# Grouped convolution by block-Toeplitz matmuls inside an FFN kernel: both parts of the conv weights in one stationary

## What is computed

```python
# x (128, 32, 512), conv weight (32, 8, 9), 4 groups of 8 channels, cond (128, 128)
out = conv1d(x, weight, padding=4, groups=4)            # along the 512 places
h = out + (cond @ c_weight.T)[:, :, None] + bias[None, :, None]
up   = h.reshape(-1, 512) @ W_up.T                       # 1376 columns
gate = silu(h.reshape(-1, 512) @ W_gate.T)
y = x + (gate * up @ W_down.T).reshape(x.shape)
```

## Time and profile before

| | us |
|---|---|
| median of 3 runs | 750.9 (750.73 to 751.24) |
| the profiled execution | 751.72 |
| its span on the core | 749.9 |
| TensorE busy | 739.6 (99%) |
| VectorE busy | 379.5 (51%) |
| ScalarE busy | 274.4 (37%) |
| granted TensorE clock | 0.999 of full |

### The profile page before, as it was taken

The page is one execution under the profiler, slowest core; times in us unless marked ns, Lnnn a source line. Parts: engine busy times, 40 slices in busy tenths (PEclk is TensorE's granted clock), DMA queues, the critical chain, the costliest instruction groups (busy, mean ns, idle before and its releaser), DMA issues.

```text
span 749.9 us, 10087 instructions
## 1 busy us (share of the span) xinstructions
PE 739.6 (99%) x3375; PEld 602.4 (80%) x3375; DVE 379.5 (51%) x639; ACT 274.4 (37%) x521; POOL 52.4 (7%) x88
## 2 busy tenths in 40 slices
PE   7999999999999999999999999999999999999998
PEld 6778888878888888887888888887888888887886
DVE  3896766654765454436734545443753333334224
ACT  4565655543433233234322333324431332333221
POOL 4433323210000000000000000000000000000000
PEclk9999999999999999999999999999999999999999
DMA  6496578569977677765544866866443967775413
GB/s 186 114 317 239 187 273 281 186 226 327 354 268 247 216 222 219 197 205 159 167 135 171 282 202 193 244 194 180 162 133 106 312 190 196 194 193 172 141 29 112
DMA packets 115029, 152.37 MB, mean 203 GB/s; under 512 B 12482, under 2 KB 50530, under 8 KB 114978
## 3 DMA queue, kind: packets, MB, share of 16 engines
q1 hardware_dynamic: 114496, 151.51, 64.8%
q10 hardware_dynamic: 482, 0.21, 0.1%
HBM read 108.95 MB, written 34.34 MB: 191 GB/s over the span
## 4 chain that ended last, share of the span: by engine, by line
PE 94%; DVE 2%; DMA 1%; SPq 1%; issue 1%; ACT 1%; POOL 0%; POOLq 0%; DVEq 0%
PE bank L727 55%; PE bank L790 32%; PE bank L645 3%; PE bank L640 3%; SPq L344 1%; PE bank L683 1%; DVE hc_lo L1091 1%; DMA x_in<-in_x 1%; PE bank L606 1%; PE bank L654 1%; PE bank L665 0%; DMA stage<-g_all 0%; DVE g_all L1294 0%; DVE ring L1091 0%; DVE g_all L1192 0%
## 5 line engine op out<-in xcount | busy, mean ns | idle before, releaser
L727 PE MATMUL bank<-hc_hi,ring 128*128 128x512 f32 (+1 forms) x1204 | 374.0, 392 | 1.0 <-issue 1.0
L727 PEld LDWEIGHTS bank<-hc_hi,ring 128*128 128x128 f32 (+1 forms) x1204 | 221.4, 185 | 50.2 <-issue 1.4
L727 PE MATMUL bank<-hc_lo,ring 128*128 128x512 f32 (+1 forms) x602 | 234.8, 390 | 0.0
L790 PE MATMUL bank<-ring,g_hi 128*128 128x512 f32 (+1 forms) x704 | 218.6, 392 | 0.0
L790 PEld LDWEIGHTS bank<-ring,g_hi 128*128 128x128 f32 (+1 forms) x704 | 131.2, 188 | 28.1 <-DVE g_lo L1091 0.8
L859 ACT ACTIVATE mix<-bank 128x512 f32<-128x512 f32 (+1 forms) x129 | 76.7, 594 | 188.0 <-PE bank L727 188.0
L790 PE MATMUL bank<-ring,g_lo 128*128 128x512 f32 (+1 forms) x352 | 137.1, 390 | 0.0
L727 PEld LDWEIGHTS bank<-hc_lo,ring 128*128 128x128 f32 (+1 forms) x602 | 111.5, 185 | 25.8
L1091 DVE TENSOR_TENSOR g_lo<-g_all,g_hi 128x512 fp32r<-128x512 f32 (+1 forms) x88 | 60.4, 689 | 88.6 <-ACT g_hi L859 88.6
L859 ACT ACTIVATE g_hi<-g_all 128x512 fp32r<-128x512 f32 (+1 forms) x88 | 55.1, 629 | 114.1 <-PE bank L790 114.0
L1265 DVE TENSOR_TENSOR mix<-bank,mix 128x512 f32<-128x512 f32 (+1 forms) x43 | 29.7, 691 | 129.4 <-PE bank L727 129.4
(11 more groups left out here) (141 smaller groups left out, 468.7 us busy)
## 6 DMA issues: line engine op xcount, KB each, us to landing
ring<-saved SPq DMA_DIRECT2D x319, 256.0 KB, 3.0
saved<-ring SPq DMA_DIRECT2D x99, 256.0 KB, 3.7
g_all<-in_x SPq DMA_DIRECT2D x32, 256.0 KB, 3.6
out_y<-g_all SPq DMA_DIRECT2D x32, 256.0 KB, 3.7
x_in<-in_x SPq DMA_DIRECT2D x96, 64.0 KB, 2.1
stage<-win SPq DMA_DIRECT2D x96, 64.0 KB, 2.9
w_nat<-in_L_ffn_W_gate SPq DMA_DIRECT2D x10, 256.0 KB, 3.4
w_nat<-in_L_ffn_W_up SPq DMA_DIRECT2D x10, 256.0 KB, 3.4
```

Of the source, the lines that this page charges most:

```text
L727: mm = pe.matmul(bank[0:w, :], wt, hv, start=fresh and q == 0 and t == 0, stop=q == 1 and t == 2, skip_group_check=not fresh)
L790: mm = pe.matmul(acc(half, tt)[:], gs, wd, start=f == 0 and t == 0, stop=f == FC - 1 and t == 2)
```

## The change

It touches groups 2 and 3 (`PAIRED = 2`); group 1 keeps its six matmuls. The stationary of 128 columns now holds the high part of the weights for 8 places of output (64 columns) and the low part of the same (64 columns): `pair_even` is high and low, `pair_odd` low and high, both views of one tile `conv_t`. For 8 places of output, 16 places of input are enough, the matmul's 128 rows. One step is two banks: `conv_ps` gets the first 8 places of each window from `x` at the window's place with `pair_even`, `xt_ps` the second 8 from `x` shifted by 8 places with `pair_odd`; each by two matmuls, one with the high and one with the low part of `x`. Half of a bank is then the part with the high weights, the other half that with the low, and VectorE adds both (and with them the fourth product, low times low, which the kernel before left out).

For that, `turn_x` transposes twice per step (at the place, and 8 places on), into `x_turn` of 1024 columns; `split_pairs` splits 1024 columns at once on both engines; `read_pairs` is four sums of 64 partitions instead of one of 128, where the third and the fourth take up what the first two wrote; `read_head` is two. `x_in` gets 8 places more on either side: rows loaded are 544 bytes instead of 512 except for the last chunk, GpSimd writes zeros at the end (`pad_x`). The paired step stands ahead of product 3, not behind it. On VectorE `read_pairs(k - 1)` and `split_pairs(k)` stand ahead of `up_b`, and `turn_x(k + 1)` behind it; on ScalarE `split_pairs` stands behind product 2's copy and the SiLU.

```diff
 def load_x(grp, i):
     if grp > 0:
+        size = P + HALO if paired(grp) and i < KC - 1 else P
...
+            def paired_step(grp, k):
+                pe.wait_ge(xt_lo_done, STEPS * grp + k + 1)
+                pe.wait_ge(conv_out, CPG * grp + k + 1)
+                for half, (bank, t) in enumerate(((conv_ps, pair_even), (xt_ps, pair_odd))):
+                    for n, v in enumerate(xt(grp)):
+                        mm = pe.matmul(bank[:], t, v[:, half * WB * P:(half + 1) * WB * P], start=n == 0, stop=n == 1)
+                mm.then_inc(conv_done, 1)
...
                     product(g, f, 2)
+                    if conv and 1 <= k <= STEPS and paired(g + 1):
+                        paired_step(g + 1, k - 1)
                     product(g, f, 3)
-                    if conv and 1 <= k <= STEPS:
+                    if conv and 1 <= k <= STEPS and not paired(g + 1):
                         conv_step(g + 1, k - 1)
...
+            def read_pairs(grp, k):
+                i = k // 2
+                if k % 2 == 0:
+                    dve.wait_ge(staged[(i - 1) % KC], STAGED * (grp if i == 0 else grp + 1))
+                dve.wait_ge(conv_done, CPG * grp + k + 2)
+                lower, upper = slice(0, HALF), slice(HALF, P)
+                halves = ((conv_ps, lower, upper), (xt_ps, upper, lower))
+                w0 = k % 2 * WB
+                to = [windows(grp, i)[mine, w0:w0 + WB, :] for _, mine, _ in halves]
+                for n, (bank, mine, other) in enumerate(halves):
+                    dve.tensor_tensor(to[n], bank[other, :].rearrange("p (w n) -> p w n", w=WB),
+                                      ctxb[other, grp:grp + 1, :].broadcast_to([HALF, WB, P]), ALU.add).then_inc(conv_lo_out, 1)
+                for n, (bank, mine, other) in enumerate(halves):
+                    dve.wait_ge(conv_lo_out, (2 * STEPS + 2) * (grp - PAIRED) + 2 * k + n + 2)
+                    last = dve.tensor_tensor(to[n], bank[mine, :].rearrange("p (w n) -> p w n", w=WB), to[n], ALU.add)
...
+            def split_pairs(grp, k):
+                dve.wait_ge(xt_hi_done, STEPS * grp + k + 1)
+                last = lo(xt_lo[:, 0:2 * WB * P], x_turn[:], xt_hi[:, 0:2 * WB * P])
...
-                    if conv and 0 <= k < STEPS:
+                    if conv and 0 <= k < STEPS and (k == 0 or not paired(g + 1)):
                         turn_x(g + 1, k)
                     gate_a(n, f)
...
+                    if conv and 1 <= k <= STEPS and paired(g + 1):
+                        read_pairs(g + 1, k - 1)
                     if conv and 0 <= k < STEPS:
-                        split_x(g + 1, k)
+                        (split_pairs if paired(g + 1) else split_x)(g + 1, k)
...
                     up_b(n, f)
...
+                    if conv and 0 <= k < STEPS - 1 and paired(g + 1):
+                        turn_x(g + 1, k + 1)
                     up_a(n, f)
```

More of the change, by code:

```diff
@@ L126, in adaln_ffn @@
         xt_lo = sb("xt_lo", [P, (2 * WB + 1) * P], F32R)
-        x_in = sb("x_in", [P, CG, P])
-        x_blk = sb("x_blk", [P, WB, R, CG])
+        x_in = sb("x_in", [P, CG, HALO + P + HALO])
+        x_turn = sb("x_turn", [P, 2 * WB * P])
         win = sb("win", [P, JJ, P])
@@ L132, in adaln_ffn, with paired @@
         toep = sb("toep", [P, G, QN, CG])
[L133 to L136, removed]
+        conv_t = sb("conv_t", [P, 4 * P], F32R)
         ident = sb("ident", [P, P])
         copy0, copy2, copy4, act_a, act_b = (mix[:, n, :] for n in range(5))
+        x_blk = x_turn[:, 0:WB * P].rearrange("n (b r c) -> n b r c", b=WB, r=R)
+        ta_hi, ta_lo, tb_hi, tb_lo = (conv_t[:, n * P:(n + 1) * P] for n in range(4))
+        PAIRED = 2
+        HALF = P // 2
+        pair_even, pair_odd = conv_t[:, 0:P], conv_t[:, HALF:HALF + P]
+        def paired(grp):
+            return grp >= PAIRED
         def down_nat(f):
@@ L206, in adaln_ffn @@
         x_turned = sem("x_turned")
+        x_padded = sem("x_padded")
+        conv_lo_out = sem("conv_lo_out")
         xt_hi_done = sem("xt_hi_done")
@@ L296, in x_place @@
         def x_place(grp, i):
-            return x_first[:, i - 1] if grp == 0 and i > 0 else x_in[:]
+            return x_first[:, i - 1] if grp == 0 and i > 0 else x_in[:, :, HALO:HALO + P]
         def blocks(grp, k):
@@ L310, in adaln_ffn @@
         NB, CQ = P // QUAD, CG // (P // QUAD)
-        x_turn = x_blk[:, :, :, :].rearrange("n b r c -> n (b r c)")
         def x_split_from(grp, k):
-            return xt_bank(grp, k)[:] if grp == 0 else x_turn
+            return xt_bank(grp, k)[:] if grp == 0 else x_turn[:, 0:WB * P]
         def xt_at(grp, k):
@@ L352, in load_x @@
                 if grp > 0:
+                    size = P + HALO if paired(grp) and i < KC - 1 else P
                     for quad in range(NB):
                         for c in range(CQ):
-                            sp.dma_start(x_in[quad * QUAD:(quad + 1) * QUAD, c::CQ, :],
-                                         x[:, grp * CG + quad * CQ + c, i * P:(i + 1) * P].rearrange("(b n) l -> n b l", b=NB)
+                            sp.dma_start(x_in[quad * QUAD:(quad + 1) * QUAD, c::CQ, HALO:HALO + size],
+                                         x[:, grp * CG + quad * CQ + c, i * P:i * P + size].rearrange("(b n) l -> n b l", b=NB)
                                          ).then_inc(x_loaded, LD)
@@ L531, in mix_t_lo, with pad_x @@
                                        ALU.subtract).then_inc(w_made[kind], 1)
+            def pad_x(grp):
+                pool.wait_ge(x_turned, STEPS * grp + STEPS - 2)
+                pool.memset(x_in[:, :, HALO + P:], 0.0).then_inc(x_padded, 1)
             def mix_h_first(q):
@@ L549, in _ @@
             pool.tensor_copy(reorder[:].rearrange("p (m r) -> p m r", r=R), ident[:].rearrange("p (r m) -> p m r", r=R)).then_inc(consts, 1)
+            pool.memset(x_in[:, :, 0:HALO], 0.0).then_inc(consts, 1)
             wrap(1)
@@ L561, in _ @@
                         mix_t_lo(f + 1)
+                    if g + 1 < G and paired(g + 1) and f == STEPS - 1:
+                        pad_x(g + 1)
         @block.tensor
@@ L629, in conv_head @@
                     pe.wait_ge(conv_out, CPG * grp)
-                for n, (t, v) in enumerate(terms(tb_hi, tb_lo, *xt(grp))):
-                    mm = pe.matmul(conv_ps[:, 0:P], t[:], v[:, 0:P], start=n == 0, stop=n == 2)
+                if paired(grp):
+                    for n, v in enumerate(xt(grp)):
+                        mm = pe.matmul(conv_ps[:, 0:P], pair_odd, v[:, 2 * WB * P:], start=n == 0, stop=n == 1)
+                else:
+                    for n, (t, v) in enumerate(terms(tb_hi, tb_lo, *xt(grp))):
+                        mm = pe.matmul(conv_ps[:, 0:P], t[:], v[:, 0:P], start=n == 0, stop=n == 2)
+                mm.then_inc(conv_done, 1)
[3 more added lines that the diff above has]
+                for half, (bank, t) in enumerate(((conv_ps, pair_even), (xt_ps, pair_odd))):
+                    for n, v in enumerate(xt(grp)):
+                        mm = pe.matmul(bank[:], t, v[:, half * WB * P:(half + 1) * WB * P], start=n == 0, stop=n == 1)
                 mm.then_inc(conv_done, 1)
@@ L870, in split_toep @@
                     act.wait_ge(toep_done, 3)
+                if paired(grp):
+                    for at in (0, P):
+                        last = hi(conv_t[:, at:at + HALF], toep[:, grp:grp + 1, HALO:2 * HALO, :])
+                    last.then_inc(t_hi_done, 1)
+                    return
                 hi(ta_hi[:], toep[:, grp:grp + 1, HALO:QN, :])
                 hi(tb_hi[:, TB0:P], toep[:, grp:grp + 1, 0:HALO, :]).then_inc(t_hi_done, 1)
+            def split_pairs(grp, k):
+                act.wait_ge(conv_done, CPG * grp + (k + 1 if k > 0 else 0))
+                act.wait_ge(x_turned, STEPS * grp + k + 1)
+                last = hi(xt_hi[:, 0:2 * WB * P], x_turn[:])
+                if k == 0:
+                    last = hi(xt_hi[:, 2 * WB * P:], head[:])
+                last.then_inc(xt_hi_done, 1)
             def split_x(grp, k):
@@ L1053, in _ @@
                         split_toep(g + 1)
-                    if conv and 0 <= k < STEPS:
+                    if conv and 0 <= k < STEPS and not paired(g + 1):
                         split_x(g + 1, k)
@@ L1061, in _ @@
                     silu_a(n, f)
+                    if conv and 0 <= k < STEPS and paired(g + 1):
+                        split_pairs(g + 1, k)
                     if n == 1:
@@ L1126, in split_toep @@
                     lo(t[2][:, R - HALO:, :], in_bank[0][:, 0:HALO, :], t[3][:, R - HALO:, :]).then_inc(t_lo_done, 1)
+                elif paired(grp):
+                    part = [conv_t[:, at:at + HALF].rearrange("p (q o) -> p q o", o=CG) for at in (0, HALF)]
+                    lo(part[1], toep[:, grp, HALO:2 * HALO, :], part[0]).then_inc(t_lo_done, 1)
                 else:
@@ L1136, in turn_x, with split_pairs @@
```

(33 more changed lines are left out.)

## The result

The changed kernel takes 752.69 us (median of 13 runs, 751.72 to 754.26) where the kernel before takes 751.34 on the same chip: ratio 1.0021, 95% interval 1.0012 to 1.0030. By the ratio that is 1.6 us slower (the two medians are 1.35 apart), where I had forecast 0.3 us faster and no measurable change. The profiled execution took 753.62 us (before 751.72), its span is 751.8 (before 749.9).

The account below looks back on a forecast made before the run. TensorE was taken as the bound. Profiled 751.7 - 7.2 (fewer matmuls) + 6.9 (stalls) = 751.4; from the median, 750.9 - 0.3 = 750.6 us, range 746.5 to 754.0.

Parts of the forecast that it names:

- the stalls behind the landing: Odd k = 3, 5, 7, both groups: product 6 waits for `up_b`, six stalls, 6.9 us.
- Gain on TensorE, 7.2 us: In groups 1 and 2, TensorE: four matmuls instead of six, 6.5 us; last step 0.6; head about 0.1.
- Even pieces hidden: Passes of the loop over `f` with even k: VectorE's chain ends at 8.83 us, product 6 due 9.11; no stall.
- Odd pieces wait for the landing: k = 3, 5, 7: `read_pairs` waits for the previous chunk's windows in `stage`; six starts sum to 32.0 us.
- The chain of 4.70 us: VectorE, from `read_pairs`' first sum to the end of `up_b`: 2.86 + 1.15 + 0.69 = 4.70 us; lower bound 4.24.
- the head loses one matmul: TensorE's head of the convolution: one matmul of 128 columns fewer, twice, about 0.1 us gained.
- signs of being wrong: Landing not last before the first sum, even pieces stalling, or the transposes being what `up_a` waits for.
- other slower ways: Slower for other reasons, such as even pieces losing their 0.3 us to spare; chance 0.04.
- 1 fell: VectorE's sums follow at 0.60 us, chain 4.24; six stalls lose 2.8 us: 747.8 us; chance 0.23.
- 2 fell: Landing of the windows doesn't matter, the whole 7.2 us stays: 743.7 us; chance 0.08.
- 3 fell: Windows' staging lands later; each 0.1 us on the average of six costs 0.6 us, e.g. 756.7; chance 0.17.
- 4 fell: Wider `x_in` rows (544 bytes) split in two, issues taking twice 0.49 us, about 1.2 us per group: 753.0; chance 0.06.

Follow-up runs that it names:

- Experiment 3: Changed kernel with the staging semaphore split in two per chunk and the convolution's head in another bank: 743.93 us, ratio 0.9897 to the kernel before.
- Experiment 5: Changed kernel with the paired step back behind product 3: 761.17 us, ratio 1.0140 to the kernel before.
- Experiments 1 and 6: Changed kernel with the staging semaphore split in two per chunk: 745.23 us; changed kernel with SyncE issuing the windows in the piece that writes them: 745.00 us.
- Experiment 4: Changed kernel with all four sums reading and writing lower halves only, leaving out work: 749.14 us, ratio 0.9965 to the kernel before.
- experiment 2: Changed kernel with the head of the convolution in another bank, so the first paired step needn't wait for it: 750.84 us, ratio 0.9988 to the kernel before.

## Why the prediction was wrong

The two large terms, TensorE's gain and the stalls behind the landing, were there and nearly cancelled, as forecast. The time was off by 1.9 us (750.6 against 1.0021 x 750.9 = 752.5), and slower instead of a little faster, because one wait was left out (item 5).

1. *Gain on TensorE, 7.2 us: right, a little small.* Even pieces went from 10.94 to 10.45, 0.49 us instead of 0.465; k = 8 gained 0.33, the head 0.1 each: 14 x 0.49 + 2 x 0.33 + 0.2 = 7.7 us. Experiment 3, without the stalls, is 7.7 us below the kernel before.
2. *Even pieces hidden: right.* 10.44 to 10.46 us, no idle TensorE. Experiment 5 shows how thin the cover is: with the step 1.36 us later each of them stalls by 1.2.
3. *Odd pieces wait for the landing: right.* First sums start 5.33, 5.77, 5.23, 5.00, 5.49 and 5.12 us into their pieces, 31.9 in all against 32.0. That the sum fits so well is luck: single starts missed my values (5.17, 5.47, 5.37, 5.17, 5.97 and 4.87) by up to 0.5 us, both ways. Experiments 1 and 6 take the landing out of the way and with it the stalls.
4. *The chain of 4.70 us: too short by 0.11.* The sums are 0.72 apart, as taken. But I let `up_b` start 0.09 before the split's end, as between full-height instructions. `up_b` starts 0.02 us behind the split's end instead: it is held as well. Experiment 4 shows that this goes with the halves that the sums use; that it comes from the bank's half read last is the rule told there, and no run varied that alone. By that rule my chain should have been 4.79 us, not 4.70. Six times 0.11 is 0.7 us. The odd pieces lost 1.30, 1.72, 1.20, 0.97, 1.46 and 1.09 us against 10.45, together 7.7, where I had 6.9. This 0.8 too little and the 0.5 too little in item 1 nearly cancelled, which is luck too.
5. *The step that failed: "the head loses one matmul", a gain of 0.1 us with nothing against it.* The paired step's wait counts `conv_out` up to k + 1, so that the first one waits for `read_head`, whose bank it writes. Before, that step stood behind product 3, 1.36 us later. `read_head`, then one instruction, ended 3.6 us into the piece, and so do its two now; what is new is that the step wants the bank earlier. The timeline of VectorE in the changed kernel, k = 1 of group 1:

```profile
240.68 0.68 DVE L1371 TENSOR_TENSOR g_all<-mix 128x512 f32<-128x512 f32 x1
241.50 0.69 DVE L1352 TENSOR_TENSOR mix<-bank,mix 128x512 f32<-128x512 f32 x1
242.22 0.29 DVE L1254 TENSOR_TENSOR head<-bank,ctxb 32x128 f32<-32x128 f32 x1
242.54 0.30 DVE L1256 TENSOR_TENSOR head<-bank,head 32x128 f32<-32x128 f32 x1
```

And that of TensorE, around its first paired matmul:

```profile
242.01 0.40 PE L760 MATMUL bank<-hc_lo,ring 128*128 128x512 f32 x1
242.98 0.47 PE L664 MATMUL bank<-xt_hi,conv_t 128*128 128x512 f32 x1 [0.58 <-DVE head L1256]
```

The matmul of product 2 that starts at 242.01 would be followed 0.23 us later, at 242.24; the next one starts at 242.98 and its successor is slow as well. k = 1 lost 0.86 and 0.83 us beyond 10.45 and the head's own 0.25: 1.7 us, and experiment 2 gave back as much in these pieces. None of my signs of being wrong looked at k = 1, and none of them came: only the 0.04 for other slower ways covers this wait. I had also put what can be told from no change at 1.5 us; the interval here is 0.7 us to either side.
6. *The rivals.* 1 fell: the sums are 0.72 apart, and experiment 4 shows what 0.60 would have given, 749.1. 2 fell, the landing matters (experiments 1, 6). 3 fell: the fourth landings were 2.9, 3.3 and 2.8 us after their issue in group 1 and 2.5, 3.0 and 2.7 in group 2, on average 2.9 as before. 4 fell: the eight `x_in` issues with 544-byte rows still take 3.91 us, and their landing 2.3 instead of 2.1 us.

The corrected sum, 751.7 - 7.7 + 7.7 + 1.7 = 753.4, stands against 753.6 for the profiled execution. Its terms are read from that execution, so it shows that nothing large is missing, not that the terms are right; for that the experiments stand. What is left, 0.2 us, is not assigned.

## What to carry to other kernels

When a step is moved ahead in one engine's order, go through every semaphore that it waits for in its new place, the first pass of the loop separately: a bank that the step shares with a smaller piece of work may have been free by a margin that the move eats. A wait that costs nothing today, hidden behind slower work, is exposed when that work gets shorter; here a semaphore that counted eight windows, when four were needed, was worth about 7.7 us once the convolution was faster (7.5 between the medians), and nothing before. Split the semaphore, or issue the transfer in the piece in which its data is ready.

## What the runs showed of the hardware

- A VectorE instruction that starts in another half of the partitions than the last one didn't overlap with it: 0.70 to 0.73 us from one to the next instead of 0.60, in 512 elements. A change of the output alone was enough: the second and the third sum both read lower halves, write the upper and the lower one, and start 0.71 us apart (267.33 and 268.04). `up_b`, back at partition 0 behind the split, paid as well (1.25 instead of 1.13).
- `gate_a` (L1352) started 0.82 us behind the instruction ahead of it (262.68 to 263.50), whose semaphore it waits for; in the kernel before, where a transpose stood between the two, it was 0.62 us behind that transpose (263.35 to 263.97). A wait for the immediate predecessor so cost about 0.2 us here, where the third and fourth sums, which wait for the one before the last, cost none in experiment 4. No run varied this alone.
- TensorE starts about 0.15 us after the end of the VectorE instruction it waits for, and two matmuls after a stop take 0.70 instead of 0.62 us, as before.
